# A feed-forward block with a conditioned LayerNorm on one core: x copied to the output's place by DMA, bias and projection added there by adding DMAs

## The reference, cut to what matters

```python
B, T, LATENT, FFN, TEMB = (4, 2048, 128, 512, 1024)
D = 8 * LATENT
xr = x.reshape(Bx, Tx, 8, LATENT)
h = jnp.einsum('btel,elf->btef', xr, W1) + b1
h = jax.nn.gelu(h, approximate=False)
y = jnp.einsum('btef,efl->btel', h, W2) + b2
y = y.reshape(Bx, Tx, Dx)
eo = jax.nn.silu(emb) @ emb_W + emb_b
scale, shift = jnp.split(eo[:, None, :], 2, axis=-1)
hn = _layernorm(y, ln_g, ln_b) * (1.0 + scale) + shift
proj = jax.nn.silu(hn) @ out_W + out_b
return x + proj
```

## Time and profile before

| | us |
|---|---|
| median of 3 runs (lowest, highest) | 727.7 (727.65, 727.92) |
| the profiled execution | 727.84 |
| its span, first to last instruction | 726.0 |
| PE busy | 720.6 (99%) |
| DVE busy | 552.2 (76%) |
| ACT busy | 453.1 (62%) |
| POOL busy | 77.9 (11%) |
| granted clock of TensorE | 1.00 |

### The profile page before, as it was taken

One profiled execution on the slowest core, in us unless ns is written; L12 is line 12 of the kernel. 1 busy time (PEld: TensorE's weight loads), 2 busy tenths in 40 slices (PEclk: granted clock), 3 DMA queues, 4 the chain that ended last, 5 costly groups with the idle time before them and its releaser, 6 DMA issues.

```text
span 726.0 us, 8305 instructions
## 1 busy us (share of the span) xinstructions
PE 720.6 (99%) x3208; PEld 585.6 (81%) x3208; DVE 552.2 (76%) x627; ACT 453.1 (62%) x494; POOL 77.9 (11%) x38
## 2 busy tenths in 40 slices
PE   8999999999999999999999999999999999999998
PEld 5887778777787888888878888888888888888886
DVE  6887888788776788889887778778778777787521
ACT  7786777767777788897865455554456453555500
POOL 0000000000000000000021221212212212122121
PEclk9999999999999999999999999999999999999999
DMA  6335366554542713323173433334332344332221
GB/s 234 110 124 187 115 219 196 181 155 164 203 152 81 261 62 113 102 72 117 59 272 133 172 117 146 116 144 175 142 148 95 137 174 170 120 117 87 87 88 58
DMA packets 42471, 101.78 MB, mean 140 GB/s; under 512 B 3136, under 2 KB 23616, under 8 KB 39360
## 3 DMA queue, kind: packets, MB, share of 16 engines
q1 hardware_dynamic: 41760, 100.73, 39.3%
q10 hardware_dynamic: 672, 0.52, 0.2%
HBM read 67.69 MB, written 33.55 MB: 139 GB/s over the span
## 4 chain that ended last, share of the span: by engine, by line
PE 98%; DMA 1%; DVE 0%; ACT 0%; issue 0%; ACTq 0%
PE psum L847 47%; PE psum L740 24%; PE psum L756 24%; PE psum L859 2%; PE psum L766 1%; DMA wraw<-in_W 1%; PE psum L781 1%; PE psum L780 1%; PE psum L803 0%; DVE g_lo L515 0%; ACT g_hi L368 0%; DVE W L491 0%; DVE res L724 0%; DVE W L489 0%; PE psum L776 0%
## 5 line engine op out<-in xcount | busy, mean ns | idle before, releaser
L515 DVE TENSOR_TENSOR g_lo<-g_raw,g_hi 128x1024 fp32r<-128x1024 f32 x128 | 156.7, 1225 | 61.3 <-ACT g_hi L368 59.0
L362 ACT ACTIVATE g_raw<-psum,cols 128x1024 f32<-128x1024 f32 x128 | 142.8, 1117 | 60.3 <-PE psum L740 51.4
L847 PE MATMUL psum<-oW_hi,s_hi 128*128 128x512 f32 x496 | 153.1, 390 | 0.0
L847 PE MATMUL psum<-oW_lo,s_hi 128*128 128x512 f32 x496 | 153.0, 389 | 0.0
L847 PE MATMUL psum<-oW_hi,s_lo 128*128 128x512 f32 x496 | 152.8, 389 | 0.0
L343 POOL TENSOR_TENSOR res<-res,out_b_all 128x1024 f32<-128x1024 f32 x32 | 77.2, 2413 | 635.7 <-DMA res<-in_x 372.9
L740 PE MATMUL psum<-xT_hi,W 128*128 128x512 f32 x508 | 137.2, 392 | 0.2
L756 PE MATMUL psum<-g_hi,W 128*128 128x512 f32 x512 | 137.3, 390 | 0.0
L740 PEld LDWEIGHTS psum<-xT_hi,W 128*128 128x128 f32 x508 | 94.2, 188 | 26.6 <-issue 7.7
L756 PEld LDWEIGHTS psum<-g_hi,W 128*128 128x128 f32 x512 | 95.9, 188 | 20.7 <-DVE yb L562 0.5
L847 PEld LDWEIGHTS psum<-oW_lo,s_hi 128*128 128x128 f32 x496 | 93.1, 188 | 19.7
(11 more groups left out here) (80 smaller groups left out, 605.6 us busy)
## 6 DMA issues: line engine op xcount, KB each, us to landing
y_scratch<-y_stage SPq DMA_DIRECT2D x32, 512.0 KB, 3.1
yb<-y_scratch SPq DMA_DIRECT2D x16, 1024.0 KB, 4.8
res<-in_x SPq DMA_DIRECT2D x32, 512.0 KB, 5.4
xT_raw<-in_xT SPq DMA_DIRECT2D x31, 512.0 KB, 4.4
out<-res SPq DMA_DIRECT2D x31, 512.0 KB, 2.8
emb_raw<-in_emb_W SPq DMA_DIRECT2D x8, 1024.0 KB, 7.5
wraw<-in_out_W SPq DMA_DIRECT2D x16, 256.0 KB, 5.0
wraw<-in_W SPq DMA_DIRECT2D x14, 256.0 KB, 4.8
```

The costliest lines, as they stand in the source:

```text
L362: nc.scalar.activation(g_raw[:, m % 2], ring(m), ACT.Gelu, bias=cols[:, R_B1 + k:R_B1 + k + 1]).then_inc(gelu_done, 1)
L515: nc.vector.tensor_tensor(g_lo[:, m % 2], g_raw[:, m % 2], g_hi[:, m % 2].bitcast(F32), ALU.subtract).then_inc(glo_done, 1)
L847: mm = nc.tensor.matmul(proj(q)[:, half], v[:, g, cut], w[:, g, half], start=(g == 0 and k == 0), stop=(g == G - 1 and k == 2))
```

## The change

- In the first stage SP issues, behind the store of y of item n, a DMA from the rows of x of tile n to the same rows of the output, in HBM (place_x). From the fifth on it first waits for the copy of four tiles earlier.
- The bias, spread over 128 partitions, is loaded at item 2. GpSimd issues 32 DMAs that add it to the output's rows, each when its copy has landed.
- In the second stage ScalarE copies the projection from PSUM to one of four buffers tile_out (take_out), which lie where res lay. GpSimd issues a DMA that adds the buffer to the output's rows.
- VectorE's additions (finish) and GpSimd's, the loads of x's rows and the plain stores go. SP's program of the second stage is only the loads of y.
- In ScalarE's program the copy of tile 2i - 1 stands ahead of the SiLUs of block i + 1, the copy of tile 2i behind the rounding of that block, ahead of the squares of the next.

```diff
@@ sync @@
-            def load_res(q):
-                sp.dma_start(res[:, q % 4], x_rows[q]).then_inc(res_landed[q % 4], 16)
+            def place_x(q):
+                if q >= 4:
+                    sp.wait_ge(x_placed[q % 4], 16 * (q // 4))
+                sp.dma_start(out_rows[q], x_rows[q]).then_inc(x_placed[q % 4], 16)
...
-                if n == Y0_ITEM + 1:
+                if n == 2:
                     sp.dma_start(out_b_all[:], out_b.rearrange("(o d) -> o d", o=1).to_broadcast([P, D])
                                  ).then_inc(out_b_landed, 16)
+                if n == Y0_ITEM + 1:
                     sp.wait_ge(emb_chunk, KE)
...
                     load_y(2)
-                    for q in range(2):
-                        load_res(q)
                 sp.wait_ge(y_staged, n + 1)
                 g, t = ORDER[n]
                 sp.dma_start(y_scratch[PT * t:PT * t + PT, :, g].rearrange("h p t -> p h t"),
                              y_stage[:, n % 2].rearrange("p (h t) -> p h t", h=PT)).then_inc(y_stored[n % 2], 16)
-
-            for q in range(2, 4):
-                load_res(q)
+                place_x(n)
+
             for s in range(2):
                 sp.wait_ge(y_stored[s], 16 * (N // 2))
-            for q in range(QN):
-                if q < QN - 1:
-                    sp.wait_ge(out_ready, q + 1)
-                    sp.dma_start(out_rows[q], res[:, q % 4]).then_inc(out_stored[q % 4], 16)
...
-                if q >= 1 and q + 3 < QN:
-                    sp.wait_ge(out_stored[(q - 1) % 4], 16 * ((q - 1) // 4 + 1))
-                    load_res(q + 3)
...
+            for p in range(4, NP):
+                sp.wait_ge(slo_done, 2 * (p - 3) + 2)
+                load_y(p)
@@ gpsimd @@
             pool.wait_ge(out_b_landed, 16)
             for q in range(QN):
-                if q == 0:
-                    pool.wait_ge(rstd_done, 2)
-                else:
-                    pool.wait_ge(proj_done, q)
-                pool.wait_ge(res_landed[q % 4], 16 * (q // 4 + 1))
-                nc.gpsimd.tensor_tensor(res[:, q % 4], res[:, q % 4], out_b_all[:], ALU.add).then_inc(res_biased, 1)
+                pool.wait_ge(x_placed[q % 4], 16 * (q // 4 + 1))
+                if q >= 4:
+                    pool.wait_ge(bias_added[q % 4], 16 * (q // 4))
+                pool.dma_start(out_rows[q], out_b_all[:], accum_op=ALU.add).then_inc(bias_added[q % 4], 16)
+            for s in range(4):
+                pool.wait_ge(bias_added[s], 16 * (QN // 4))
+            for q in range(QN - 1):
+                pool.wait_ge(out_ready, q + 1)
+                pool.dma_start(out_rows[q], tile_out[:, q % 4], accum_op=ALU.add).then_inc(out_added[q % 4], 16)
+            for h in range(2):
+                half = slice(h * BANK, (h + 1) * BANK)
+                pool.wait_ge(out_ready, QN + h)
+                pool.dma_start(out_rows[QN - 1, :, half], tile_out[:, (QN - 1) % 4, half], accum_op=ALU.add
+                               ).then_inc(out_added[(QN - 1) % 4], 16)
+            for s in range(4):
+                pool.wait_ge(out_added[s], 16 * (QN // 4 + (s == (QN - 1) % 4)))
@@ scalar @@
+            def take_out(q):
+                act.wait_ge(proj_done, q + 1)
+                if q >= 4:
+                    act.wait_ge(out_added[q % 4], 16 * (q // 4))
+                nc.scalar.copy(tile_out[:, q % 4], proj(q)).then_inc(out_ready, 1)
...
             for i in range(NP - 1):
                 p = i + 1
+                if i > 0:
+                    take_out(2 * i - 1)
                 for h in range(2):
                     act.wait_ge(normed, 2 * p + h + 1)
...
                     round_s(p, h)
+                take_out(2 * i)
                 if p + 1 < NP:
                     square(p + 1, 0)
...
+            take_out(QN - 3)
+            take_out(QN - 2)
+            act.wait_ge(out_added[(QN - 1) % 4], 16 * (QN // 4 - 1))
+            for h in range(2):
+                half = slice(h * BANK, (h + 1) * BANK)
+                act.wait_ge(proj_done, QN + h)
+                nc.scalar.copy(tile_out[:, (QN - 1) % 4, half], proj(QN - 1)[:, half]).then_inc(out_ready, 1)
@@ vector @@
-            def finish(q):
-                dve.wait_ge(proj_done, q + 1)
-                dve.wait_ge(res_biased, q + 1)
-                nc.vector.tensor_tensor(res[:, q % 4], proj(q), res[:, q % 4], ALU.add).then_inc(out_ready, 1)
...
-                if i > 0:
-                    finish(2 * i - 1)
...
-                finish(2 * i)
...
-            dve.wait_ge(res_biased, QN)
-            for h in range(2):
-                half = slice(h * BANK, (h + 1) * BANK)
-                dve.wait_ge(proj_done, QN + h)
-                nc.vector.tensor_tensor(res[:, (QN - 1) % 4, half], proj(QN - 1)[:, half], res[:, (QN - 1) % 4, half],
-                                        ALU.add).then_inc(out_ready, 1)
```

More of the change, by code:

```diff
@@ L128, in cond_ffn_program @@
         s_lo1 = at("s_lo1", [P, G, TP], R0 + 24 * KB, F32R)
-        res = at("res", [P, 4, D], R0 + 48 * KB)
+        tile_out = at("tile_out", [P, 4, D], R0 + 48 * KB)
         yb2 = at("yb2", [P, G, TP], R0 + 64 * KB)
@@ L200, in cond_ffn_program @@
         out_b_landed = sem("out_b_landed")
-        res_landed = [sem(f"res_landed{s}") for s in range(4)]
-        res_biased = sem("res_biased")
+        x_placed = [sem(f"x_placed{s}") for s in range(4)]
+        bias_added = [sem(f"bias_added{s}") for s in range(4)]
         out_ready = sem("out_ready")
-        out_stored = [sem(f"out_stored{s}") for s in range(4)]
+        out_added = [sem(f"out_added{s}") for s in range(4)]
         def pair(b):
@@ L302, in _ @@
                              y_stage[:, n % 2].rearrange("p (h t) -> p h t", h=PT)).then_inc(y_stored[n % 2], 16)
-            for q in range(2, 4):
-                load_res(q)
+                place_x(n)
             for s in range(2):
                 sp.wait_ge(y_stored[s], 16 * (N // 2))
-            for q in range(QN):
-                if q < QN - 1:
-                    sp.wait_ge(out_ready, q + 1)
-                    sp.dma_start(out_rows[q], res[:, q % 4]).then_inc(out_stored[q % 4], 16)
-                else:
-                    for h in range(2):
-                        half = slice(h * BANK, (h + 1) * BANK)
[L315 to L320, removed]
-                if q >= 1 and q + 3 < QN:
-                    sp.wait_ge(out_stored[(q - 1) % 4], 16 * ((q - 1) // 4 + 1))
-                    load_res(q + 3)
-            for s in range(4):
-                sp.wait_ge(out_stored[s], 16 * (QN // 4 + (s == (QN - 1) % 4)))
+            for p in range(4, NP):
+                sp.wait_ge(slo_done, 2 * (p - 3) + 2)
+                load_y(p)
         @block.gpsimd
```

## The result

The changed kernel takes 764.67 us (median of 4 runs, 759.49 to 767.06), the kernel before 727.73: a ratio of 1.050, with a 95% interval of 1.046 to 1.053. Forecast were 766 us, slower, with 738 to 797. The profiled execution took 765.78 us; its span is 763.7, 37.7 more than the span of before.

The account below looks back on a forecast made before the run. The prediction took TensorE to bound the kernel (busy 720.6 of 726.0 us), with a first-stage DMA loop close behind. 727.84 + 36.6 for copies + 2.0 for the end, less 0.1, gave 766 us, range 738 to 797.

Parts of the forecast that it names:

- The loop with 0.44 us to spare: First stage: cast, staging and store of y, load of x, next cast need 10.44 us of a 10.88 us turn.
- D = 2.3: First stage: us each copy of x adds ahead of the x load; 36.6 us in all after TensorE's lead.
- the row taken as nearest, 205 GB/s: Profile row where a store gives way to a load on q1; as a bound it gives 2.56 us per copy.
- The bias adds cost nothing, their load under 1 us: First stage: GpSimd's 32 adds start after x has moved, so cost nothing; the bias load costs under 1 us once.
- the second rival: First stage: copies and bias adds fill the 16 DMA engines, 15 us more, total 781 or 797; chance 0.15.
- The three kinds of turn: First stage, 29 loads: 11 with weights only, 8 with embedding, 10 late; 20.5, 5.0 and 13.0 us longer.
- VectorE's additions and ScalarE's copies cost nothing: Second stage: 38.0 us of VectorE additions go, 34.7 us of ScalarE copies come, none of it on the path.
- The end, +2.0: Kernel's end: the last adding DMA of 256 KB lands in 4.0 us in place of a store's 2.0.
- the casts' waits: First-stage sign: the cast of x waits for its DMA in nearly every item, some 1 to 2 us.
- The rival in which only the end gets longer: Copy and load packets overlap until D is under 0.44, first stage unchanged, 730 us; chance 0.05.
- the one that isn't slower: Same overlap of copy and load, and the last adding DMA lands like a plain store; 728 us; chance 0.06.
- The fast copy: First stage: the copy goes at the load's rate, D = 1.34 to 1.6, total 741 to 747; chance 0.22.

Follow-up runs that it names:

- e7: Changed kernel with every copy of x made twice, the second into a scratch tensor, ahead of the load of x: 810.45 us.
- e9: Changed kernel with each copy issued behind the next load of x and the bias adds moved to the second stage: 733.39 us.
- e10: Changed kernel with each tile of x loaded one item earlier, its copies and adds left as they are: 734.76 us.
- e2: Changed kernel without the 32 bias adds; the bias load, copies and second stage stay: 748.06 us.
- e5: Changed kernel without the 32 copies of x; each bias add waits for its item's store of y instead: 738.61 us.
- e3: Changed kernel with the bias loaded ahead of item 0 in place of item 2: 757.39 us.
- e8: Changed kernel with the second stage's adding DMAs of GpSimd replaced by plain stores of SP: 757.88 us.
- e4: Kernel before the change, with the bias loaded by one plain DMA from GpSimd's queue in place of SP's: 728.09 us.

## Why the prediction was right

The total was 1.3 us off, and the sign and the mechanism were right: a copy in line ahead of the load of x, in a loop with next to nothing to spare. That the total came out so close is luck. Of the span's 37.7 us the forecast had 22.9 too many for the copies, and 16.5 too few for the bias adds, 4.2 for the end and 1.3 for the second stage, and these errors cancel. By its steps:

- *The loop with 0.44 us to spare.* Right, and shown from three sides: e7 (each microsecond in line costs a microsecond a load), e9 and e10 (out of the line, or the loop opened, the first stage is back).
- *The copy's price, D = 2.3, and 36.6 us for it.* Too dear. D measured 1.6 (e2), the copies alone 13.7 us. By the forecast's own sums D = 1.6 gives 16.9, so the turns were summed about right and D was mis-sized: the packets are of 32 KB, and the row taken as nearest, 205 GB/s, had the turn from store to load in it. The Trainium skill's 207 to 214 GB/s for copies between HBM tensors ("DMA: Bandwidth & Descriptors", Latency and other measured facts), by which D would be 2.5 (an estimate), don't carry over to this copy: counted by what it delays, 512 KB in 1.6 us are 328 GB/s. The page took them on tiles of 128 x 16 KiB whose rows lie 512 KiB and more apart, a condition that the forecast left out; here all rows are contiguous.
- *The bias adds cost nothing, their load under 1 us.* Wrong, and this made up for D. Alone they cost 4.1 us, all of it where two are issued together after the bias has landed (e5, e3), and with the copies they make up the other 16.5 of 30.2. "Each starts when its copy has landed, so after the x tile has been moved" is true, but what they then delay is the rest of the burst. In the changed kernel the embedding's load lands 9.2 us after its issue (7.5 before), so the next store, copy and load of x start behind it:

```profile
emb_raw<-in_emb_W SPq DMA_DIRECT2D x1, 1024.0 KB, 10.0
...
xT_raw<-in_xT SPq DMA_DIRECT2D x1, 512.0 KB, 6.1
...
out<-out_b_all POOLq DMA_DIRECT2D x1, 512.0 KB, 8.6
...
out<-in_x SPq DMA_DIRECT2D x1, 512.0 KB, 6.8
xT_raw<-in_xT SPq DMA_DIRECT2D x1, 512.0 KB, 7.4
```

  The first three rows are of an item with an embedding load (10.0 us to landing beside an add of 8.6), the last two of the item after it: the copy lands after 6.8 us in place of 4.6 and x after 7.4 in place of 6.1. The embedding's load is issued at 177.6 and so lands at 187.6, the next store is issued at 187.19. That is the second rival's contention, and near its price (15 us), but it acts through the loop and not by full engines: e10 moves the same bytes, and its first stage takes 367.1 us. Both queues do run on the same 16 engines: from 187 to 200 us of the changed kernel q1 takes 50.0% of them and q0 32.6%. But SP's queue isn't sure of a share: from 44.6 to 48.2 us of the changed kernel GpSimd's queue alone moves packets (104.7% of the 16 engines), while the store issued at 45.28 waits. In what share the 16.5 us divide between such items, the bunch (e3 gives 7.3 for it) and the clock after it is known only to a few us, since the four executions of the changed kernel lie 7.6 us apart.
- *The three kinds of turn.* The 11 turns with weights and no embedding were to get longer by 1.86, the 8 with an embedding by 0.63, the late ones by 1.3. Measured on the average, the first by 2.1 (10.8 to 13.0, the bunch among them), the second by -0.2 (12.2 to 12.0), the third by 0.9 (11.1 to 12.0). The long turns moved to the items after those with an embedding.
- *VectorE's additions and ScalarE's copies cost nothing.* Right: TensorE has 40.00 of 40 us in the second stage, and e8 shortens it by 0.2 only. That the 1.3 us at its beginning come from copies and adds still in the queues is not shown: e2, e5 and e9 have only one of the two in the first stage, and in each the second takes 355.6, but e7 has both and takes 355.9.
- *The end, +2.0.* Too small: 6.2. The landing was as forecast (3.7 for 4.0), and GpSimd's DRAIN of 4.19 us was not in the sum (e8).

Of the signs, the casts' waits came as forecast (56.0 us in 28 of them, 2.0 each), but x landed 5.7 us after its issue and not 7, and TensorE's idle time in the first stage grew by 19.4 us and not by 37: its busy time grew by 10.8, of which the clock explains some 1.6, and the rest stays open.

The rival in which only the end gets longer, 730 us, and the one that isn't slower are excluded by the first stage. The fast copy (D from 1.34 to 1.6) was right about the copy and wrong in the total.

## What to carry to other kernels

An engine at 99% doesn't say that nothing else is critical: look for loops that go through a DMA queue, and sum what is spare in one turn. Here 0.44 us in 10.88 stood between a kernel that hides 33.6 MB of new traffic in its first stage (32 copies and 32 adds of 512 KB; 101.78 to 118.55 MB in the whole run) and one that loses 30 us to it. Issue a load when its buffer comes free, ahead of waits and stores that it doesn't need, and look first at what stands in line ahead of it. And count what an engine must still do after its last DMA.

## What was not expected of the hardware

- A copy of 512 KB from HBM to HBM, both sides contiguous, went as 16 packets of 32 KB, one for each DMA engine, and took 1.6 us of the line.
- An adding DMA out of SBUF into HBM moved its 4 KB packets in 0.35 us, twice the time of a load's; 512 KB landed 5.3 us after the issue, 256 KB after 3.7, with 0.86 us of GpSimd's time for each.
- With 32 or more adding DMAs issued by GpSimd, its closing DRAIN took 2.7 to 4.2 us after the last of them had landed: 2.68 us in e8 (32 such DMAs), 2.76 in e2 (33), 3.21 in e9 and 4.19 in the changed kernel (65 in both). Without any, and with one plain DMA (e4), it went beside GpSimd's last addition and ended with it to within 0.2 us. So it isn't the number of DMAs alone, and its cause stays open. It costs time only where GpSimd is among the last to finish.
